# A recurrent block and cross-attention on one core: two operands moved to PSUM, the first layer norm one period earlier, and a new order of work

## The reference

```
xa = ln(x);  sx = shifted(xa) - xa;  xxx = xa + sx * maa_x
m = adapters(tanh(xxx @ maa_w1))               # five: w, k, v, r, g
xj = xa + sx * (maa_j + m_j)                   # for j in w, k, v, r, g
w = exp(-exp(time_decay + tanh(xw @ decay_w1) @ decay_w2))
r, k, v = xr @ Wr.T, xk @ Wk.T, xv @ Wv.T;  g = silu(xg @ Wg.T)
for each token:  a = k v^T;  y = r (faaaa * a + s);  s = a + w * s
y = group_norm(y) * gn_w + gn_b                # per head
x = x + (y * g) @ Wo.T
xc = ln(x);  sxc = shifted(xc) - xc            # channel mix
rr = sigmoid((xc + sxc * fmaa_r) @ fWr.T)
kk = relu((xc + sxc * fmaa_k) @ fWk.T) ** 2
x = x + rr * (kk @ fWv.T)                      # the latents
```

## Time and profile before

| | us |
|---|---|
| runs of the kernel before | 1056.35, 1060.24, 1061.8; median 1060.24 |
| the profiled execution, its own time | 1062.83 |
| its span, first to last instruction | 1061.1 |
| mean granted TensorE clock in it | 0.942 |
| start of L576 in periods 1 to 7 | 91.2, 145.9, 198.9, 252.5, 305.5, 358.7, 411.7 |

### The profile page before, as it was taken

The page is one execution under the profiler, slowest core; times in us unless marked ns, Lnnn a source line. Parts: engine busy times, 40 slices in busy tenths (PEclk is TensorE's granted clock), DMA queues, the critical chain, the costliest instruction groups (busy, mean ns, idle before and its releaser), DMA issues.

```text
span 1061.1 us, 17589 instructions
## 1 busy us (share of the span) xinstructions
PE 927.3 (87%) x6888; PEld 712.9 (67%) x6888; DVE 602.8 (57%) x1298; ACT 424.4 (40%) x957; POOL 227.4 (21%) x231
## 2 busy tenths in 40 slices
PE   4775788888888888679699999999999978999998
PEld 4664566666666666346478778787787846888886
DVE  2567889888989898962213432332343245545543
ACT  4111223232323233343265656666565556333332
POOL 2427344444444445400000000000000002000100
PEclk8876998989898989898899999999999989999999
DMA  6466333323242324100700101101010023000101
GB/s 223 115 204 225 131 104 79 105 70 114 76 145 73 110 69 107 53 18 1 272 1 8 52 3 54 46 9 47 8 54 1 10 86 127 0 0 27 43 0 35
DMA packets 34618, 77.10 MB, mean 73 GB/s; under 512 B 12590, under 2 KB 18734, under 8 KB 33519
## 3 DMA queue, kind: packets, MB, share of 16 engines
q1 hardware_dynamic: 34542, 76.07, 22.9%
HBM read 68.72 MB, written 7.34 MB: 72 GB/s over the span
## 4 chain that ended last, share of the span: by engine, by line
PE 51%; issue 21%; POOL 14%; DMA 5%; DVE 5%; ACT 3%; SPq 1%; POOLq 0%; DVEq 0%; ACTq 0%
POOL scan L450 9%; PE bank L1452 8%; PE bank L1575 8%; PE bank L1563 7%; PE bank L1446 6%; PE bank L1526 4%; PE bank L1467 3%; PE bank L1221 3%; PE bank L1518 3%; POOL xj L441 3%; DMA scan<-v_scratch 2%; PE bank L1548 2%; PE bank L1227 2%; PE bank L1481 2%; DMA v_scratch<-vt 1%
## 5 line engine op out<-in xcount | busy, mean ns | idle before, releaser
L749 DVE CUSTOM_DVE_ANT_0 smb<-bank,mask 112x487 f32<-112x487 f32 x128 | 78.6, 660 | 119.4 <-issue 119.4
L560 DVE TENSOR_TENSOR_SCAN scan<-bank,scan 128x448 f32<-128x448 f32 x128 | 132.1, 1073 | 9.9 <-POOL scan L453 9.9
L1221 PE MATMUL bank<-xj,front 128*128 128x112 f32 x1024 | 127.3, 287 | 11.1 <-POOL xj L441 11.1
L1221 PEld LDWEIGHTS bank<-xj,front 128*128 128x128 f32 x1024 | 124.6, 203 | 14.2 <-POOL xj L441 9.2
L450 POOL TENSOR_TENSOR scan<-scan,ks 128x896 f32<-128x896 f32 x64 | 125.7, 1964 | 26.1 <-DMA scan<-v_scratch 26.1
L1094 ACT ACTIVATE smb<-smb,nmax 112x487 f32<-112x487 f32 x128 | 88.5, 694 | 84.3 <-DVE nmax L749 84.3
L427 POOL TENSOR_TENSOR small<-small,neghalf 112x1 f32<-112x1 f32 x24 | 14.3, 594 | 475.3 <-DVE small L773 311.8
L567 DVE TENSOR_TENSOR scan<-scan,bank 128x896 f32<-128x896 f32 x64 | 69.4, 1084 | 3.1 <-DVE scan L560 0.5
L1526 PE MATMUL bank<-ident,smb 112*122 112x112 f32 x512 | 59.4, 265 | 4.7 <-ACT smb L1094 3.9
L1446 PE MATMUL bank<-cx_hi,kw_hi 128*128 128x488 f32 x128 | 53.1, 415 | 9.8 <-DVE cx_lo L639 9.8
L441 POOL TENSOR_TENSOR xj<-tmp,xa 128x448 f32<-128x448 f32 x40 | 41.6, 1058 | 90.9 <-DVE tmp L529 90.9
(11 more groups left out here) (180 smaller groups left out, 1946.2 us busy)
## 6 DMA issues: line engine op xcount, KB each, us to landing
scan<-v_scratch SPq DMA_DIRECT2D x64, 448.0 KB
w<-in_w SPq DMA_DIRECT2D x2, 4096.0 KB, 12.8
cx<-in_ctxt SPq DMA_DIRECT2D x8, 750.0 KB, 5.4
raw_w<-in_wbig SPq DMA_DIRECT2D x1, 4096.0 KB, 21.7
tail<-in_wbig SPq DMA_DIRECT2D x1, 3072.0 KB
front<-in_wbig SPq DMA_DIRECT2D x2, 1024.0 KB, 10.2
x_f<-in_x SPq DMA_DIRECT2D x8, 224.0 KB, 3.7
v_scratch<-vt SPq DMA_DIRECT2D x32, 56.0 KB, 1.8
```

The source lines that it names most:

```text
L560: n = v.tensor_tensor_scan(flat, decay, flat, 0.0, ALU.mult, ALU.add)
L749: v.tensor_tensor_reduce(sm[r], bank[r][0:T, 0:NKEY], mask_b[b % 2][:, :], -1.0 / DH, 3e38, ALU.add, ALU.min, nmax[:, h:h + 1]).then_inc(s ...
L1221: i = t_.matmul(tiles(dst)[:, m, :], w[:, k, m * P:(m + 1) * P], x[:, k, :], start=k == 0, stop=k == NT - 1)
```

## The change

- `sx_t` becomes four tiles of PSUM bank 4. `gstd` keeps only the deviation; its inverse, `grec`, lies in bank 4, columns T to 2T.
- The first layer norm of sequence d + 1 is done at the end of the preceding period: its start ahead of scan 6, its end ahead of `times_r` 7, POOL's part behind scan input 7. Period −1 does sequences 0 and 1.
- `hidden_keys` writes to bank 5 instead of 4, so `hidden_gate`, which also writes bank 5, waits for ACT's relu.
- The order changes on DVE (scan 1 ahead of `centred`, `shift` ahead of `own_token`, `gating` after scan 2, scan 6 ahead of mix R and G), on ACT (`input_columns` first, `latent_columns` ahead of `norm_weights`) and on PE (receptance and `input_turned` ahead of the means, `adapter_inputs` ahead of `own_sums`, the adapters V, K, W ahead of `block_output`).

```diff
-        sx_t = room.take("sx_t", [P, NT, T])
-        gstd = room.take("gstd", [P, 2, T])
+        gstd = room.take("gstd", [P, T])
...
+        sx_t = tiles(4)
+        grec = bank[4][:, T:2 * T]
...
# POOL, period(i)
-                if real(d):
-                    rstd(1, d)
+                if i == -1:
+                    rstd(1, 0)
                 if real(b):
                     for n in (2, 3, 4, 5):
                         scan_input(b, n)
...
                     scan_input(b, 7)
+                if real(d + 1):
+                    rstd(1, d + 1)
...
# DVE, group_norm
-                v.reciprocal(gstd[:, 1, :], gstd[:, 0, :]).then_inc(s["grstd"], 1)
+                v.reciprocal(grec, gstd[:, :]).then_inc(s["grstd"], 1)
                 dve.wait_ge(s["grstd"], b + 1)
-                v.tensor_tensor(y_cen[:, :, :], y_cen[:, :, :], per_head(gstd[:, 1, :]), ALU.mult
+                v.tensor_tensor(y_cen[:, :, :], y_cen[:, :, :], per_head(grec), ALU.mult
...
# DVE, period(i), its second half
                     times_r(b, 5)
+                if real(d + 1):
+                    norm_first(d + 1)
+                if real(b):
+                    scan_chunk(b, 6)
                 if real(d):
                     mix(d, MIX_R)
                     mix(d, MIX_G)
                 if real(b):
-                    for n in range(6, NCH):
-                        scan_chunk(b, n)
-                        times_r(b, n)
+                    times_r(b, 6)
+                    scan_chunk(b, 7)
+                if real(d + 1):
+                    norm_end(1, rows_f, x_f, "xn_ready", d + 1)
+                if real(b):
+                    times_r(b, 7)
...
# ACT, period(i)
+                if real(d):
+                    input_columns(d)
                 if real(a_):
                     squares(a_)
                 if real(b):
                     decays(b, 1)
                 if real(a_):
                     deviation(a_)
-                    norm_weights(a_)
-                if real(b):
-                    gate_tanh(b)
                 if real(before):
                     latent_columns(before)
+                if real(a_):
+                    norm_weights(a_)
+                if real(b):
+                    gate_tanh(b)
                 if real(d):
-                    input_columns(d)
...
# PE
-                to_columns(4, W["fWk"], xk[:, 0], "kkp_ready")
+                to_columns(5, W["fWk"], xk[:, 0], "kkp_ready")
...
                 pe.wait_ge(s["xk_ready"], 2 * b + 2)
+                pe.wait_ge(s["kk_relu"], b + 1)
                 to_rows(5, W["fWr"], xk[:, 1], "rrp_ready")
```

More of the change, by code:

```diff
@@ L508, in norm_start, with norm_first @@
                                 ).then_inc(s[f"ve{n}"], 1)
+            def norm_first(d):
+                dve.wait_ge(s["xf_loaded"], 16 * (d + 1))
+                norm_start(1, x_f, d)
             def norm_end(n, dst, src, done, b):
@@ L649, in period @@
                 before, a_, b, d = i - 2, i - 1, i, i + 1
+                if i == -1:
+                    norm_first(0)
+                    norm_end(1, rows_f, x_f, "xn_ready", 0)
+                if real(b):
+                    scan_chunk(b, 0)
                 if real(a_):
@@ L652, in period @@
                 if real(b):
-                    scan_chunk(b, 0)
+                    scan_chunk(b, 1)
                 if real(a_):
@@ L657, in period @@
                     latents(before)
-                if real(b):
-                    scan_chunk(b, 1)
                 if real(d):
-                    dve.wait_ge(s["xf_loaded"], 16 * (d + 1))
-                    norm_start(1, x_f, d)
+                    shift(d)
                 if real(b):
@@ L673, in period @@
                     out_bias()
-                if real(d):
-                    norm_end(1, rows_f, x_f, "xn_ready", d)
                 if real(b):
                     times_r(b, 1)
+                    scan_chunk(b, 2)
                     gating(b)
-                    scan_chunk(b, 2)
                 if real(a_):
                     gated(a_)
-                if real(d):
-                    shift(d)
                 if real(b):
@@ L945, in deviation @@
                 act.wait_ge(s["gvar"], b + 1)
-                c_.activation(gstd[:, 0, :], var_bank, ACT.Sqrt, bias=eps[:, :]).then_inc(s["gsd"], 1)
+                c_.activation(gstd[:, :], var_bank, ACT.Sqrt, bias=eps[:, :]).then_inc(s["gsd"], 1)
             def norm_weights(b):
@@ L967, in relu_squares @@
                 wait(act, "ffn_ready", b)
-                c_.activation(kk[:, :, :], tiles(4), ACT.Relu).then_inc(s["kk_relu"], 1)
+                c_.activation(kk[:, :, :], tiles(5), ACT.Relu).then_inc(s["kk_relu"], 1)
                 act.wait_ge(s["kk_relu"], b + 1)
@@ L1010, in period @@
                     deviation(a_)
+                if real(before):
+                    latent_columns(before)
+                if real(a_):
                     norm_weights(a_)
@@ L1013, in period @@
                     gate_tanh(b)
-                if real(before):
-                    latent_columns(before)
                 if real(d):
-                    input_columns(d)
                     if d == 0:
@@ L1379, in period @@
                 before, a_, b, d = i - 2, i - 1, i, i + 1
+                if real(b):
+                    receptance_product(b)
+                if real(d):
+                    input_turned(d)
                 if real(a_):
@@ L1390, in period @@
                 if real(d):
-                    input_turned(d)
+                    adapter_inputs(d)
                 if real(b):
@@ L1394, in period @@
                     sum_pair(b, 0)
+                if real(d):
+                    adapters(d, (MIX_V, MIX_K, MIX_W))
                 if real(a_):
                     block_output(a_)
-                if real(d):
-                    adapter_inputs(d)
-                    adapters(d, (MIX_V, MIX_K, MIX_W))
                 if i == B - 1:
```

4 lines of the change are left out of this document (1 added, 3 removed).

## The result

| | before | after |
|---|---|---|
| median, us | 1059.26 | 1080.18 |
| runs | 1056.35 to 1061.8 (4) | 1076.87 to 1081.63 (4) |
| profiled execution | 1062.83 | 1080.34 |

The change makes the kernel slower: the ratio is 1.018, 95% interval 1.0149 to 1.021, some 20 us. The direction was forecast, the size (1068) was not; the measured time lies at the upper edge, just outside the range.

A forecast was written before the change was run, and what follows sets the result against it. No engine is full; a period is a cycle through several, mainly DVE then PE. 50.0 plus (c) 1.9, (d) 1.7, (e) 0.9 gave 54.5 against 53.57; 5.5 in six periods, 7.7 in total: 1068, range 1046 to 1080.

The forecast's parts named there:

- (e): V product at the start of PE's run: a low clock there costs 0 to 1.85 us a period, taken as 0.9.
- (d): Wo's eight matmuls on PE: a fall of the clock there costs 0 to 2.7 us a period, taken as 1.7.
- Segment 1: DVE's part of a period, from centred to mix V's end: 26.3 us before, 19.05 after removals, then new waits added.
- (a): Gate on DVE: the product of scan 1 and scan 2 now lie in between, leaving 0.6 us of wait.
- (b): Wo on PE now follows the three adapters, 4.8 us at full clock against 4.0 of DVE work: 0.9 of wait.
- (c): POOL's scan inputs 4 and 5 beside latents, shift and the four L520 on DVE: 0 to 3 us, taken as 1.9.
- Segment 2: PE's part, mix V's end to next centred: 29.42 us at full clock, 2.1 more, with receptance ahead of the means.
- Rival 4: The clock falls by Wo's start and returns for the whole V product: 1079 to 1086, say 1082; chance 0.13.
- Rivals 1 to 3: Clock does not fall, 1051 (chance 0.20); POOL's inputs miss latents and shift, 1056 (0.17); neither cost, 1039 (0.05).
- Rival 1: TensorE's clock does not fall in the broken-up pauses: period 51.9, time 1051; chance 0.20.
- Rival 5: An operand in PSUM does not free L587, the product with the inverse deviation: +1.47 a period, 1077; chance 0.05.
- Edits with one answer: Channel mix's difference in PSUM: nothing, or 1.9 if DVE were late; hidden_keys in bank 5: 0.7 at the tail.

The follow-up runs named there:

- e9_fill_v: Changed kernel plus unread TensorE matmuls in periods 1 to 6, 9 behind Wo and 3 ahead of the V product: 1066.9, ratio 1.005 to the kernel before.
- e10_fill_wo: Changed kernel plus unread TensorE matmuls only ahead of Wo (6 and 6) in periods 1 to 6: 1068.8, ratio 1.009 to the kernel before.
- e5_fill2: Changed kernel plus unread matmuls: 6 ahead of sum pair 0, 6 behind it, 9 after Wo, 3 ahead of V: 1056.4, ratio 0.992 to the kernel before.
- e4_grec: Kernel before with one edit, the inverse deviation in PSUM bank 4: 1053.2, ratio 0.994.
- e8_sxt: Kernel before with the channel mix's difference in PSUM bank 4, hidden keys in bank 5 and hidden gate behind the relu: 1067.0, ratio 1.0035.
- e12_norm: Kernel before with both PSUM edits and the first norm moved to the preceding period's end, otherwise in the old order: 1055.2, ratio 0.994.
- e11_best: Changed kernel, means and variances earlier on PE, scan inputs 2 to 5 held until xxx, unread matmuls ahead of adapters, after Wo, ahead of V: 1033.1, ratio 0.975.

## Why the prediction was wrong

- **The step that failed: term (e), the price of a low clock under the V product.** The prediction put it at 0.9, between 0 and 1.85. The run of V and K took 2.9 longer in the mean and 2.6 to 3.1 in each of the six periods; e9_fill_v, with the pauses ahead of it filled, has 7.40 in all six. K took its usual 3.74 and V all of the extra: 6.65 instead of 3.65. So the bound named the right product at the wrong price. 1.85 is half of the 3.7 us that V takes at full clock, but a product at half clock takes nearly twice its time (the first half of V took 3.55, where 1.88 is usual), so by these figures the bound is near its whole length, an estimate of 3.5. The prediction's own rows had it: Wo, as long at full clock, took 6.39 in rows 9, 2.7 more, and that price was used for (d).
- **A second mistake beside it.** (d) and (e) were weighed as one fall that comes beside Wo or beside V, each at a middle value. The new order has two groups of pauses, and e9_fill_v and e10_fill_wo show that each has its own fall. With 2.9 for (e) the forecast of a period would have been 56.5; 56.3 was measured.
- **From the period to the time.** The period is 1.8 above the forecast of 54.5: 2.0 by (e), less 0.2 elsewhere. That is 11 of the 12 us between 1068 and 1080.2, but the rest agrees by luck. Six periods grew by 17.4 in the profiled executions where 5.5 was forecast; outside them nothing was added where 2.2 was forecast; and the forecast moved by 2.6 from the profiled execution to the median, where the changed kernel's own lay 0.2 above its median: 11.9 − 2.2 + 2.4 = 12.
- **Segment 1: right.** Forecast 24.2, measured 24.1, and term by term: (a) 0.6, measured 0.54; (b) and (d) together 2.6, measured 2.8 in the mean, from 0.9 to 3.9; (c) 1.9, measured 2.0, from 0.2 to 3.6. Its upper bound of 3, two waits of 1.47, was passed in one period, since a DVE operation can wait for nearly the whole of a scan input (a single xxx took 1.95, where 0.33 is usual).
- **Segment 2 without the clock: right.** Forecast 29.4; e5_fill2 and e9_fill_v, which differ from the changed kernel by the fillers alone, have 29.2. `centred` waited 2.33 ("about 2").
- **Rival 4** had both falls, one at Wo and one over the whole V product, and V at the same wrong price: 1079 to 1086. Wo cost 1.6 to 2.0 in five periods and nothing in one, where it had 2.7; V cost 2.9, where it had 1.85. That its time is near the measured one is the sum of two misses. The condition it named, that PE be idle enough between own sums and adapters, is borne out by e10_fill_wo for Wo; the fall under V goes with the pauses behind Wo instead.
- **Rivals 1 to 3** are refuted as forecasts of this kernel. Rival 1's time (1051) was that of the changed kernel with the clock up, and e5_fill2 bears it out: its ratio of 0.992 to the kernel before is 1052 on the prediction's scale. Rival 5 is refuted by e4_grec: the product takes 0.62 beside a running scan input.
- **Two rules, against the traces.** The Trainium skill (SBUF — State Buffer, "Who interferes with whom") says that a VectorE operation with two SBUF inputs contends with a GpSimd one that reads SBUF, and that one with at most one SBUF input, outside the 2-port modes, does not. The traces agree in both directions: the product of e4_grec and the eight xk, with one input in SBUF and one in PSUM, are free beside a scan input, L527 and L629 with two in SBUF are not. The advice of the Trainium skill to leave no long gap between bursts (TensorE: Matmul & The Clock Gate, "Why this matters for your kernels") must not be read gap by gap: pauses of 2.93 and 0.92 to 1.07 with 1.5 of work between were followed by 0.50 in all six periods, and filling 2.1 and 0.9 of them (e5_fill2, e9_fill_v) kept it at 1.00.
- **Edits with one answer.** The channel mix's difference saves nothing: shown by e8_sxt. The moved norm was put at −1.47 in segment 1 and nothing in segment 2; e12_norm has −0.5 and +0.4. In the sum of the changed kernel this did not show, as scan 2 covers the gate's wait there.
- **Around the periods.** Last period +1.2 for the +2 forecast (centred to centred, 48.15 to 49.33). Behind its end 1.4 were saved, where 0.7 more was forecast. The first `whole_y` stood 2.6 earlier, where −0.5 was forecast, but the first `centred` waited 3.05 and stood 0.2 later. In the profiled executions of the changed kernel and the four with fillers alone, which are the same program up to there, the first `whole_y` lies between 88.3 and 95.2, so nothing is concluded from it.

## What to carry to other kernels

Price a fall of TensorE's clock by what a product of the same length cost in a trace at the low clock (here 2.7 to 3.0 for 3.7 us of work, not 1.85), laid on whatever is critical where it would start, and count a fall for each group of pauses, not for each kernel. Before a VectorE operation with two SBUF inputs is moved, look at what GpSimd does at the new place: in the kernel before, POOL's scan inputs stood behind the first norm, which looked like a loss, and `latents` met none of them; with the norm moved it met one in e12_norm (1.58 for 0.69), and in the changed order shift and xxx met them as well. Put first on an engine what another engine will wait for: with the means ahead of the receptance product, the variances ahead of the gate product and POOL's scan inputs 4 and 5 held, the change gained 1.2% instead of losing 1.8%, and with unread products in two pauses 2.2%.

## What was not expected of the hardware

- Unread matmuls paid: 24 per period, 5.8 us of PE time, took 27 us off the changed kernel (1.018 to 0.992); the granted clock stayed at 1.00 through Wo, V and K. In e11_best one period of six had V and K at 9.2 in spite of them.
- The port is taken in turns: with four short DVE operations against two POOL ones, the DVE ones waited twice, 1.95 and 1.85 for 0.33 each, and POOL's L454 took 1.07 instead of 0.21, through the end of one DVE operation and the whole of the next (L524).
- An operation with one SBUF input can wait for POOL too, where it is a `tensor_scalar` from SBUF to SBUF: L513 in e4_grec, 1.35 for 0.53. The prediction's "two SBUF inputs" was too narrow. The Trainium skill (SBUF — State Buffer, "Who interferes with whom") names `tensor_scalar` among the operations that can enter a 2-port mode and so contend; which mode L513 ran in no run shows.
- The first `whole_y` moved by 7 us between profiled executions of programs that are the same up to there.
